# Linear attention and a mixture of experts in one kernel: chunks of 64 keys, paired A V groups, a product as the mask, and another order around the experts' start

## The reference

```python
q, k, v = split_heads(xn @ Wq), split_heads(xn @ Wk), split_heads(xn @ Wv)   # 16 heads: q, k of 16, v of 8
A = (q / 4 @ k.T) ** 2 * causal          # the scan over chunks of 64 tokens is the same as all 256 at once
x = x + merge_heads((A @ v) / (A.sum(-1) + 1e-5)) @ Wo
scores = softmax(layernorm(x) @ gate_w + gate_b)         # 8 experts, the 2 best are kept
# each token's result is that of the kept expert with the highest number:
y = relu(layernorm(x) * score @ w1[e] + b1[e]) @ w2[e] + b2[e]
x = x + y
```

## Time and profile before

| | |
|---|---|
| median of 3 runs | 302.42 us (302.14 to 303.39) |
| profiled execution | 301.87 us, span 299.8 us |
| PE busy | 264.3 us (88%) |
| PEld busy | 206.5 us (69%) |
| DVE busy | 188.2 us (63%) |
| ACT busy | 168.0 us (56%) |
| POOL busy | 166.1 us (55%) |
| granted clock of TensorE, mean | 0.975 |
| first square of scores | 15.70 us |
| first and last relu of the experts | 210.91 and 289.35 us |

### The profile page before, as it was taken

One profiled execution on the slowest core, in us unless ns is written; L12 is line 12 of the kernel. 1 busy time (PEld: TensorE's weight loads), 2 busy tenths in 40 slices (PEclk: granted clock), 3 DMA queues, 4 the chain that ended last, 5 costly groups with the idle time before them and its releaser, 6 DMA issues.

```text
span 299.8 us, 9144 instructions
## 1 busy us (share of the span) xinstructions
PE 264.3 (88%) x3141; PEld 206.5 (69%) x3141; DVE 188.2 (63%) x726; ACT 168.0 (56%) x297; POOL 166.1 (55%) x190
## 2 busy tenths in 40 slices
PE   1989999999998998998999999853999999999980
PEld 1756676676666676665766766522998888999970
DVE  5561552794795695696585587993577845555550
ACT  2266667667665665575676665632464645556620
POOL 6064453653866675676566566842175764445551
PEclk9999999999999999999999999995799999999996
DMA  5799999996000000000000000085375369766200
GB/s 155 213 350 365 358 358 360 358 357 201 20 3 20 0 20 21 2 18 20 3 21 17 3 20 20 29 252 135 96 168 163 113 191 284 216 184 180 96 24 0
DMA packets 31580, 40.58 MB, mean 135 GB/s; under 512 B 3330, under 2 KB 24356, under 8 KB 31536
## 3 DMA queue, kind: packets, MB, share of 16 engines
q1 hardware_dynamic: 29264, 35.76, 39.2%
q0 software_dynamic: 2272, 4.25, 4.1%
HBM read 17.98 MB, written 22.48 MB: 135 GB/s over the span
## 4 chain that ended last, share of the span: by engine, by line
PE 61%; DVE 21%; ACT 8%; issue 4%; DMA 1%; SPq 1%; POOLq 0%; DVEq 0%; POOL 0%; ACTq 0%
PE sc L990 24%; PE p L990 19%; PE av L990 14%; ACT scores L404 7%; PE p L993 4%; DVE shifted L723 2%; DVE k_sb L658 1%; DVE stats L607 1%; DVE ahead L732 1%; DVE t_row L857 1%; DVE o_sb L680 1%; DVE stats L695 1%; DMA rows<-in_L_attn_hidden_states 1%; SPq L304 1%; DVE rden L677 1%
## 5 line engine op out<-in xcount | busy, mean ns | idle before, releaser
L404 ACT ACTIVATE scores<-sc 128x1536 f32<-128x1536 f32 x64 | 92.9, 1451 | 53.9 <-PE sc L990 53.9
L524 POOL TENSOR_SCALAR_AFFINE_SELECT scores<-scores 128x1024 f32<-128x1024 f32 x64 | 71.1, 1112 | 62.5 <-ACT scores L404 62.3
L990 PE MATMUL sc<-q_sb,k_sb 32*128 32x256 f32 (+1 forms) x1024 | 60.4, 350 | 7.0 <-ACT scores L404 6.8
L990 PEld LDWEIGHTS sc<-q_sb,k_sb 32*128 32x128 f32 x1024 | 47.4, 186 | 25.0 <-issue 14.9
L990 PE MATMUL av<-scores,v_ext 128*32 128x256 f32 (+1 forms) x1024 | 54.9, 332 | 0.0
L562 POOL DMA_INDIRECT out<-y_sb,xr x39 | 38.5, 986 | 29.5 <-DVE y_sb L932 23.4
L472 ACT ACTIVATE hT<-sc,b_sb 128x128 f32<-128x128 f32 x78 | 24.4, 363 | 35.2 <-PE sc L990 35.2
L990 PE MATMUL sc<-xwT,w_t 128*128 128x128 f32 x312 | 42.9, 283 | 0.0
L549 POOL DMA_INDIRECT expert_rows<-rows,slot_i x32 | 32.8, 1026 | 16.7 <-DVE slot_i L803 9.3
L920 DVE TENSOR_SCALAR hT<-sc,b_sb 128x128 f32<-128x128 f32 x78 | 23.8, 347 | 27.1 <-PE sc L990 24.8
L990 PEld LDWEIGHTS sc<-xwT,w_t 128*128 128x128 f32 x312 | 39.6, 199 | 0.0
(11 more groups left out here) (136 smaller groups left out, 344.0 us busy)
## 6 DMA issues: line engine op xcount, KB each, us to landing
expert_rows<-pad_rows SPq DMA_DIRECT2D x11, 1572.0 KB, 17.8
w_t<-in_L_ffn_w SPq DMA_DIRECT2D x39, 256.0 KB
xr<-expert_rows SPq DMA_DIRECT2D x39, 65.5 KB, 2.4
rows<-in_L_attn_hidden_states SPq DMA_DIRECT2D x16, 128.0 KB, 2.8
out<-y_sb,xr POOLq DMA_INDIRECT x39, 2.9
b_sb<-in_L_ffn_b SPq DMA_DIRECT2D x1, 512.0 KB, 4.4
expert_rows<-rows,slot_i POOLq DMA_INDIRECT x32
wk_sb<-in_L_attn_Wk SPq DMA_DIRECT2D x1, 128.0 KB, 2.5
```

Source lines behind the costliest of these rows:

```text
L404: nc.scalar.activation(scores[g][:, :, :, :].rearrange("p c a t -> p c (a t)"), sc[:, :, 0:SW], ACT.Square, scale=Q_SCALE).then_inc(square ...
L524: nc.gpsimd.affine_select(out=scores[g][:, :, 0:2, :], in_=scores[g][:, :, 0:2, :], compare_op=ALU.is_ge, fill=0.0, base=0, pattern=[[0, G ...
L990: return nc.tensor.matmul(o, lhsT=l, rhs=r, start=start, stop=stop)
```

## The change

1. Scores are made for 64 keys of two heads at once (`STAGES`): the stationary operand is 2 x 64 columns of the one `k_sb`, where the two copies of k lie side by side for each chunk. An even group takes chunks s = 0 and 2, an odd one s = 1 and 3; it has 320 columns instead of 384. Inputs are loaded in chunks so that partitions 0 to 63 hold chunks 0 and 3 and the others 1 and 2; V is projected to both halves of the partitions by eight products instead of two, into `values`, and Wv is loaded in two parts, by even and odd heads.
2. The mask is a product with a 0/1 tile `causal` over 128 of the 320 columns, instead of a select over 256 of 384.
3. Order: A V of two groups directly behind each other; q and k projections together; `exponent` ahead of the first square; the choice ahead of the keys in DVE's list; in the last period two scatters and a root ahead of the first mask.
4. The first table's tiles lie in PSUM (`table_parts` on p6, which is idle then; the second table's on p7); `first_left` is somewhat shorter.
5. Around the experts' start: SP issues four `w1` ahead of the rows instead of six, the rows of the second wave ahead of its weights; the last batch's transposes, division and prefix go behind the first tiles' work; registers for the second wave are loaded three tiles earlier on ACT and DVE.

```diff
+    CHUNK = 64
+    NC = L // CHUNK
+    STAGES = (((0, 0, 4, 1), (2, 2, 1, 0)), ((1, 1, 3, 2), (3, 2, 2, 0)))
+    CUT = (0, 1)
+    SW = 5 * CHUNK
+    HW = H // 2 * HD
...
+        VW = HW + E
+        values = p7[:, 0:NC * VW].rearrange("p (s d) -> p s d", s=NC)
+        counted = p7[:, NC * VW:NC * VW + (PT + 1) * E]
...
-                sp.dma_start(rows[:, b, :, 0:D], x[b].rearrange("(j p) d -> p j d", p=P)).then_inc(x_in[b], 16)
+                chunks = x[b].rearrange("(s p) d -> p s d", p=CHUNK)
+                sp.dma_start(rows[0:CHUNK, b, :, 0:D], chunks[:, 0:4:3, :]).then_inc(x_in[b], 16)
+                sp.dma_start(rows[CHUNK:P, b, :, 0:D], chunks[:, 1:3, :]).then_inc(x_in[b], 16)
...
+            heads = Wv.rearrange("p (h r d) -> p r h d", r=2, d=HD)
+            for r, at in ((0, 0), (1, VW)):
+                sp.dma_start(wv_sb[:, at:at + HW].rearrange("p (h d) -> p h d", d=HD), heads[:, r, :, :]
+                             ).then_inc(attn_w, 16)
...
-            for t in range(W1):
+            row = loaded(sp, row_i[0][0:1, 0:WAVE], E * REGION)
+            for t in range(4):
                 load_w1(t, e[t])
-            row = loaded(sp, row_i[0][0:1, 0:WAVE], E * REGION)
             sp.wait_ge(rows_out[0], 16 * EARLY * PT)
             for t in range(WAVE):
                 load_rows(t, row[t])
-            for t in range(W1, WAVE):
+                if t in (3, 5):
+                    load_w1((t + 5) // 2, e[(t + 5) // 2])
+            for t in range(W1, WAVE - 1):
                 load_w1(t, e[t])
-            e = experts(sp, 1)
-            load_w1(WAVE, e[0])
-            row = loaded(sp, row_i[1][0:1, 0:TILES - WAVE], E * REGION)
+            e = e + experts(sp, 1)
+            SOON = 6
+            row = row + loaded(sp, row_i[1][0:1, 0:SOON], E * REGION)
             sp.wait_ge(rows_out[1], 16 * (NP - EARLY) * PT)
-            LEAD = 3
-            for t in range(WAVE, WAVE + LEAD):
-                load_rows(t, row[t - WAVE])
-            for t in range(WAVE, TILES):
-                if t + LEAD < TILES:
-                    load_rows(t + LEAD, row[t + LEAD - WAVE])
-                if t > WAVE:
-                    load_w1(t, e[t - WAVE])
+            for t in range(WAVE, WAVE + 2):
+                load_rows(t, row[t])
+            load_w1(WAVE - 1, e[WAVE - 1])
+            row = row + loaded(sp, row_i[1][0:1, SOON:TILES - WAVE], E * REGION)
+            for t in range(WAVE + 2, TILES):
+                load_rows(t, row[t])
+                load_w1(t - 2, e[t - 2])
+            for t in range(TILES - 2, TILES):
...
+            for half in range(2):
+                part, far = slice(half * CHUNK, (half + 1) * CHUNK), 1 - half
+                pool.wait_ge(pool_step, 4 + half)
+                nc.gpsimd.affine_select(out=causal[part, :], in_=causal[part, :], compare_op=ALU.is_ge, fill=0.0,
+                                        base=0, pattern=[[0, 2], [1, CHUNK]], channel_multiplier=-1)
+                nc.gpsimd.iota(rows[part, :, :, IDCOL].bitcast(i32), pattern=[[L, NB], [(1 + 2 * far) * CHUNK, NTK]],
+                               base=half * CHUNK, channel_multiplier=1).then_inc(pool_step, 1)
+            pool.wait_ge(pool_step, 6)
...
-                nc.gpsimd.affine_select(out=scores[g][:, :, 0:2, :], in_=scores[g][:, :, 0:2, :],
-                                        compare_op=ALU.is_ge, fill=0.0, base=0,
-                                        pattern=[[0, GH], [0, 2], [1, P]], channel_multiplier=-1).then_inc(masked, 1)
+                cut = scores[g][:, :, CUT[g % 2] * CHUNK:(CUT[g % 2] + 2) * CHUNK]
+                nc.gpsimd.tensor_tensor(cut, cut, causal[:, :].unsqueeze(1).broadcast_to([P, GH, 2 * CHUNK]),
+                                        ALU.mult).then_inc(masked, 1)
...
+                if p == NB:
+                    scatter(send)
+                    scatter(send + 1)
+                    norm2_root(logits)
...
+                if choice is not None:
+                    exponent(choice)
                 if core is not None:
                     square(core, 0)
-                if choice is not None:
-                    exponent(choice)
...
-            exponent(NP - 2)
             act.wait_ge(b1_done, 1)
             nc.scalar.copy(b1_sb[:, :], xw_bank[:, 0:E * FC]).then_inc(b1_ready, 1)
-            copy_u(NB - 1)
             e = experts(act, 0)
-            copy_oT(NB - 1)
-            for t in range(3):
-                normalise(t)
+            normalise(0)
+            normalise(1)
             copy_xwT(0)
             copy_xwT(1)
+            copy_u(NB - 1)
+            normalise(2)
...
-                    ins = nc.vector.tensor_scalar(k_sb[b % 2][r][:, :], p5[:, :], parity[:, r:r + 1], None, ALU.mult)
+                    ins = nc.vector.tensor_scalar(k_sb[b % 2][:, :, r, :], p5[:, :].rearrange("p (s k) -> p s k", k=CHUNK),
+                                                  parity[:, r:r + 1], None, ALU.mult)
...
+                    part, gate = slice(r * CHUNK, (r + 1) * CHUNK), HW * (1 - r)
                     nc.vector.tensor_copy(
-                        v_ext[b % 2][:, :, r, :, SUB * r:SUB * r + HD],
-                        projected[:, :, 0:D].rearrange("p j (x r d) -> p j x r d", r=2, d=HD)[:, :, :, r, :])
-                nc.vector.tensor_tensor(raw_x[:, b, :, :], projected[:, :, D:DE],
-                                        std1[:, b, :].unsqueeze(2).broadcast_to([P, NTK, E]),
-                                        ALU.mult).then_inc(v_ready, 1)
+                        v_ext[b % 2][part, :, :, SUB * r:SUB * r + HD],
+                        values[part, :, E * r:E * r + HW].rearrange("p s (h d) -> p s h d", d=HD))
+                    ins = nc.vector.tensor_tensor(raw_x[part, b, :, :], values[part, r:NC:2, gate:gate + E],
+                                                  std1[part, b, :].unsqueeze(2).broadcast_to([CHUNK, NTK, E]), ALU.mult)
+                ins.then_inc(v_ready, 1)
...
+            def table_parts(bank):
+                at, parts = 0, []
+                for shape in ((E,), (E,), (E,), (E + 1,), (WIDE,), (WIDE, E), (WIDE,), (WORDS, PACK), (WORDS,), (WIDE,)):
+                    n = math.prod(shape)
+                    ap = bank[0:1, at:at + n]
+                    parts.append(ap if len(shape) == 1 else ap.rearrange("p (a b) -> p a b", b=shape[1]))
+                    at += n
+                return parts
...
+            first, second = table_parts(p6), table_parts(p7)
             for p in PERIODS:
                 if p == NB:
-                    first_counts()
-                    tiles_before()
-                    tiles_passed()
-                    tiles_packed()
-                    table_done(0, tile_row)
+                    first_counts(first)
+                    tiles_before(first)
+                    tiles_passed(first)
+                    tiles_packed(first)
+                    table_done(first, 0, tile_row)
                 new, late, tail, nxt = of(p, 0), of(p, LATE), of(p, TAIL), of(p, -1)
                 stats, logits, choice = pair_of(p, -4), pair_of(p, LOGITS), pair_of(p, CHOICE)
+                if choice is not None:
+                    route_sum(choice)
+                    route_score(choice)
+                    route_onehot(choice)
+                if new is not None:
+                    part_k(new)
                 if tail is not None:
                     residual(tail)
                     norm2_stats(tail)
                 if p == NB:
-                    first_left()
-                if choice is not None:
-                    route_sum(choice)
-                    route_score(choice)
-                    route_onehot(choice)
+                    first_left(first)
...
-            def route_late(t):
+            def late_piece(t):
                 k = NP - 1
                 if t == 0:
+                    divide(NB - 1)
+                    route_place(k - 1)
+                    route_taken(k - 1)
+                if t == 1:
+                    route_rows(k - 1)
...
-                q, k, at = q_sb[b % 2], k_sb[b % 2][g % 2], (g // 2) * L
-                for c in range(GH):
-                    strip = slice(STRIP * c, STRIP * (c + 1))
-                    mm(sc[:, c, P:SW], k[strip, at:at + P], q[strip, at:at + L])
-                for c in range(GH):
-                    strip = slice(STRIP * c, STRIP * (c + 1))
-                    last = mm(sc[:, c, 0:P], k[strip, at + P:at + L], q[strip, at + P:at + L])
+                q, k, half = q_sb[b % 2], k_sb[b % 2], g // 2
+                for s, query, n, at in STAGES[g % 2]:
+                    for c in range(GH):
+                        strip = slice(STRIP * c, STRIP * (c + 1))
+                        lo = half * L + query * CHUNK
+                        last = mm(sc[:, c, at * CHUNK:(at + n) * CHUNK],
```

(61 more changed lines are left out.)

187 lines of the change are left out of this document (88 added, 99 removed).

## The result

The change makes the kernel slower: 319.08 us (317.78 to 320.72, four runs) against 302.42 us (302.14 to 303.39, three runs), a ratio of 1.0546, 95% interval [1.0476, 1.0615]. A fourth execution of the kernel before took 616.66 us, twice the others, and is not used. The profiled execution took 317.78 us with a span of 316.0. I had predicted 286.4 us.

The account below looks back on a forecast made before the run. TensorE's own work was taken as the limit in attention and experts. Attention -9.4, turn -7.2, second table -0.8 and start +1.4 gave -16.0 us against the profiled 301.87, forecast 286.4 us, range 279.5 to 295.

Parts of the forecast that it names:

- the start: Kernel start: GpSimd's mask and numbering setup delays its first root, +1.4 us (+0.8 to +1.8).
- the second input load: At the start: issued 0.5 us later on SP, said to end behind GpSimd's delay.
- the periods with a choice: Attention periods with the router's choice: VectorE decides, 10.75 us undisturbed, 12.1 disturbed, 11.7 taken with two of three disturbed.
- The mask's length: GpSimd's mask product in attention: 512 elements of two operands, 1.1 us taken, GpSimd staying hidden.
- the turn: From attention to experts: earlier first expert product and full clock, -7.2 us (-3.5 to -9).
- The durations on TensorE at full clock: Attention blocks, start to start: scores' groups 0.81 and 0.76 us, A V 0.67, V 0.64.
- The periods without a choice: Attention periods without the router's choice: TensorE's 10.10 us plus 0.2 for small waits, 10.3 against 11.24.
- The experts: Expert stage: second table's rows ahead of weights and register loads three tiles earlier, -0.8 us (0 to -1.5).
- (c): Rival in attention: two-operand mask makes GpSimd the bound, passing TensorE at 1.6 us a mask; 315 us, chance 0.06.
- (a): Rival in attention: VectorE keeps the gain, all choice periods disturbed at 12.3 us; 289 to 300 us, chance 0.25.
- The last sign of being wrong: In choice periods: the first square waiting long for `exponent` would show the forecast wrong; no size given.

Follow-up runs that it names:

- b1: Kernel before with each of its 16 x loads issued as two of 64 partitions, nothing else: 326.76 us against 314.0 for the kernel before.
- e1: Kernel after with pad transfers issued between later x loads, experts' weight loads last: 316.23 us where before takes 314.0; attention 174.7 us.
- e4: e1 with the row scatter behind mask 3 instead of ahead of it: 311.66 us against 315.9 for the kernel before; attention 168.7 us.
- b2: All of the change except the 64-key chunks (scores, V, mask, x loads as before): ratio to the kernel before 0.9771.
- b3: b2 plus the scatter behind mask 3 and SyncE's list for the experts as before: 293.21 us against 301.85, ratio 0.9708.
- e7: e4 with SyncE's list for the experts as before the change: 300.67 us against 301.85 for the kernel before.
- e5: e1 with the mask as one select of 512 elements, triangle partly wrong: 297.69 us against 315.9 for the kernel before; attention 161.2 us.

## Why the prediction was wrong

**Step that failed first: the start.** It counted "the second input load (0.5 us later on SP)" for one load. The change has two issues for each of sixteen loads, and SyncE's queue runs on to the pads and from there to the first scatter. Doing this alone costs 12 us of attention (b1), and undoing it in the kernel after gains 16.6 (e1), 10.9 of them in the seventh period. I had the price of an issue; I never asked what stands last in that queue and who waits for it.

**Second: the periods with a choice.** I took 11.7 us, with 1.4 us for one held-up operation in two of three. The four later ones were 15.5 on average. The mask's length was off by little (1.1 taken, 1.27 measured), but three things were missing. First, the operation beside two masks in a row waits for both (3.13 us, not 1.66), and whether masks stand in a row depends on where the scatter stands: with the scatter behind mask 3 (e4) `ahead` and `best` are at 0.43 and 0.19 us and the period is 11.65. The trace before had shown it once, in `t_row`'s 2.61 us from 189.74, beside two selects in a row:

```profile
190.15 2.17 POOL L524 TENSOR_SCALAR_AFFINE_SELECT scores<-scores 128x1024 f32<-128x1024 f32 x2
```

Second, three operations of one choice are held up, not one; together with the first this makes 4.6 us, which the residual hands on to TensorE as a wait of 4.57. Third, the forecast has a price for TensorE's clock in the turn and none in the attention, where each of these waits is followed by 3 to 6 us at 1.2 GHz.

The Trainium skill (SBUF — State Buffer, Who interferes with whom) says that a VectorE instruction with two SBUF inputs contends with a GpSimd one that reads SBUF. The trace agrees: `ahead` ends at 145.25, behind the second of two masks that ran from 142.46 to 144.97 us.

**What held.** The durations on TensorE at full clock: from start to start the scores' groups are 0.81 and 0.76 us as predicted, a pair of A V groups 1.22 (2 x 0.67 = 1.34 predicted), V 0.64; the square 1.24 (1.23), V's copies 0.42:

```profile
133.09 0.83 PE L1038 MATMUL sc<-q_sb,k_sb 32*128 32x192 f32 x16
133.85 1.29 PE L1038 MATMUL av<-scores,v_ext 128*32 128x256 f32 x32
135.07 0.73 PE L1038 MATMUL p<-wo_sb,oT 128*128 128x136 f32 x4
135.73 0.88 PE L1038 MATMUL sc<-q_sb,k_sb 32*128 32x256 f32 x16
136.54 0.70 PE L1038 MATMUL p<-wv_sb,xnT 128*64 128x72 f32 x16
137.18 0.55 PE L1041 MATMUL p<-ident,u_sb 128*128 128x128 f32 x3
```

The periods without a choice came out at 10.5 on average (10.3). The start is +1.25 (+1.4): GpSimd's first root has its first operation at 5.09 us and the second at 5.41. The turn is -8.0 (-7.2): the first expert product starts at 222.68, 15.4 us after the last batch's first scores at 207.28 (14.9 predicted), at full clock, and no operation of the first table takes over 0.35 us; b2 and b3 show a gain of 5 to 6 us without the rest.

**The experts** were to gain 0.8 and lost 2.7. The product of tile 17 waits for its weights, which the new list issues late:

```profile
262.51 1.16 PE L1038 MATMUL sc<-xwT,w_t 128*128 128x128 f32 x8 [2.26 <-DMA w_t<-in_L_ffn_w]
```

That is 2.3 of it; that the list causes it is argued, not shown (e7).

**The rivals.** The result lies on the side of (c), yet by another way: GpSimd is not the bound (4 x 1.27 + 3.9 = 9.0 us a period), and the mask stayed below the 1.6 us at which (c) has it pass TensorE. (a) had the place right, VectorE in the choice periods, with a price of 12.3 where 15.5 came. No rival had a late transfer. The last sign of being wrong, a long wait of the first square for `exponent`, did not come: in the period shown above ScalarE waited 0.89 us for `exponent`'s input, up to 141.79.

## What to carry to other kernels

When a change splits a transfer, count its issues over all batches and follow that queue to its end: what stands last, and which wait on which engine it feeds. Where two engines hold each other up, look at how long the other's instructions run without a gap at the place where yours are issued: moving one unrelated instruction, the scatter, was worth 6.0 us of attention (e4), against 13.5 for halving the mask's time (e5). And a wait costs more than its length where the clock is low behind it. Test a bundle in parts: what gained here (the turn to the experts and the order of the lists, 3% together with the moved scatter) was buried under late pads and a longer mask, in five periods that are 27 us longer than before.

## What the runs showed that I had not expected

- A VectorE operation of two operands waits out two GpSimd instructions in a row, 3.13 us for 0.42 us of work, not only the one beside it.
- On GpSimd the select takes 641 ns for 512 elements and 1112 for 1024, the product 1273 for 512: half the elements cost more than all of them did. The Trainium skill (GPSIMD Engine Reference, Performance versus the Vector engine) has about 2.6 cycles an element for two operands, from which my estimate was 1.1 us. The trace has 0.17 us more. The select's two lengths leave as much for an instruction without elements: 512 elements more cost 471 ns, and 641 - 471 = 170 ns.
- A transfer into 64 partitions takes 0.61 us to issue, one of the same tensor into 128 partitions 0.47.
- On three chips the experts took some 10 us longer than in the other runs, for every kernel, with the attention the same. TensorE waits there for the normalised rows (6.4 us in b2 between 190 and 250 us); why these come later is open.
